# Moving a rank-16 side product out of the up-projection loop of a fused transformer layer, and spreading that loop over four PSUM banks

## The reference, cut to what matters

```python
def qat_lora_linear(x, W, b, A, B):
    Wq = fake_quant_weight(W)              # symmetric 8-bit rounding of the weights
    base = jnp.einsum('bsi,oi->bso', x, Wq) + b
    lora = jnp.einsum('bsr,or->bso', jnp.einsum('bsi,ri->bsr', x, A), B)
    return base + SCALING * lora
h = qat_lora_linear(hidden_states, W_fc, b_fc, A_fc, B_fc)
h = jax.nn.gelu(h, approximate=False)
h = qat_lora_linear(h, W_proj, b_proj, A_proj, B_proj)
...
x = _layernorm(x + attn(x)); x = _layernorm(x + ffn(x))
```

## Time and profile before

| | us |
|---|---|
| three timed runs | 2717.56, 2712.26, 2716.21; median 2716.21 |
| the profiled execution | 2710.28 |
| its span, core 4 (the slowest; the cores have 2699.1 to 2708.6) | 2708.6 |
| PE busy / weight loads / DVE busy / ACT busy in the span | 1614.0 / 757.8 / 1018.9 / 882.2 |
| mean granted TensorE clock, cores 0 to 7 | 0.658 to 0.664 |

### The profile page before, as it was taken

One profiled execution on the slowest core, in us unless ns is written; L12 is line 12 of the kernel. 1 busy time (PEld: TensorE's weight loads), 2 busy tenths in 40 slices (PEclk: granted clock), 3 DMA queues, 4 the chain that ended last, 5 costly groups with the idle time before them and its releaser, 6 DMA issues.

```text
span 2708.6 us, 28767 instructions; the slowest of 8 cores (2699.1 to 2708.6 us)
## 1 busy us (share of the span) xinstructions
PE 1614.0 (60%) x7027; PEld 757.8 (28%) x7038; DVE 1018.9 (38%) x1325; ACT 882.2 (33%) x1229; POOL 74.2 (3%) x119
## 2 busy tenths in 40 slices
PE   0255666677766345412244768677676766777666
PEld 0111222222222112100122435344353433435334
DVE  2266777777777644565544100101000010100101
ACT  0002666666666133512665211112111121211211
POOL 0000000000000000000000000000000000000000
PEclk9667888888797577556555757556575665756557
DMA  5400121211213222201322000000000000000000
GB/s 158 130 1 6 55 66 55 69 55 56 68 51 131 86 75 66 75 0 52 100 96 70 16 1 1 16 0 16 1 1 16 1 16 0 9 8 1 16 1 16
DMA packets 51903, 112.32 MB, mean 41 GB/s; under 512 B 12656, under 2 KB 23408, under 8 KB 50464
## 3 DMA queue, kind: packets, MB, share of 16 engines
q0 software_dynamic: 13552, 50.08, 5.7%
q1 hardware_dynamic: 28688, 37.06, 4.6%
q10 hardware_dynamic: 9504, 23.34, 2.9%
HBM read 97.47 MB, written 8.39 MB: 39 GB/s over the span
## 4 chain that ended last, share of the span: by engine, by line
PE 41%; DVE 21%; ACT 17%; issue 10%; DMA 9%; ACTq 1%; DVEq 1%; SPq 0%; POOLq 0%
PE PSD L313 32%; DVE CL L692 5%; ACT HH L1133 5%; ACT PT L699 4%; PE PSD L1142 3%; DVE MXW L565 3%; ACT QSG L802 3%; PE BIG L608 2%; DMA QSG<-wPRr 2%; DVE CL L685 2%; PE PSD L676 2%; DMA QSG<-wFCr 2%; ACT QTI L806 2%; DMA out<-OST 1%; DMA STG<-xT 1%
## 5 line engine op out<-in xcount | busy, mean ns | idle before, releaser
L313 PE MATMUL PSD<-XT,RTF 128*128 128x256 bf16 x2048 | 482.0, 417 | 1.3 <-DVE UO L1101 1.2
L699 ACT ACTIVATE PT<-CL 128x1024 bf16<-128x1024 f16 (+1 forms) x320 | 310.8, 971 | 184.4 <-DVE CL L685 94.1
L1133 ACT ACTIVATE HH<-PSD,BFCS,SML 128x256 bf16<-128x256 f32 x256 | 144.4, 564 | 672.7 <-PE PSD L313 669.7
L1142 PE MATMUL PSD<-HH,APT 128*16 128x256 bf16 x256 | 94.9, 371 | 397.3 <-ACT HH L1133 353.4
L313 PEld LDWEIGHTS PSD<-XT,RTF 128*128 128x128 bf16 x2048 | 264.6, 140 | 162.4 <-issue 66.7
L1153 DVE TENSOR_SCALAR UPt<-PSD,SML 16x256 bf16<-16x256 f32 x8 | 3.8, 472 | 741.3 <-PE PSD L1142 741.3
L676 PE MATMUL PSD<-QH,KH 96*128 96x512 bf16 (+3 forms) x640 | 199.3, 403 | 114.9 <-DVE CL L685 53.2
L692 DVE TENSOR_SCALAR CL<-PSD 128x1024 f16<-128x1024 f32 x192 | 235.0, 1224 | 74.7 <-PE BIG L608 32.8
L313 PE MATMUL PSD<-HH,RTP 128*128 128x256 bf16 x2048 | 250.7, 284 | 6.4 <-DVE UPt L1153 6.4
L608 PE MATMUL BIG<-PT,VP 128*65 128x512 bf16 (+3 forms) x640 | 196.4, 394 | 68.0 <-ACT PT L699 54.4
L313 PEld LDWEIGHTS PSD<-HH,RTP 128*128 128x128 bf16 x2048 | 202.8, 102 | 45.7 <-issue 8.6
(11 more groups left out here) (148 smaller groups left out, 1294.9 us busy)
## 6 DMA issues: line engine op xcount, KB each, us to landing
STG<-wFCr POOLq DMA_DIRECT2D x32, 512.0 KB, 4.3
STG<-wPRr POOLq DMA_DIRECT2D x32, 512.0 KB, 4.4
out<-OST SPq DMA_DIRECT2D x64, 128.0 KB, 1.9
QSG<-wFCr ACTq DMA_DIRECT2D x27, 256.0 KB, 2.6
QSG<-wFCr POOLq DMA_DIRECT2D x26, 256.0 KB, 2.9
QSG<-wPRr SPq DMA_DIRECT2D x22, 256.0 KB, 3.1
QSG<-wPRr POOLq DMA_DIRECT2D x21, 256.0 KB, 2.8
QSG<-wPRr ACTq DMA_DIRECT2D x21, 256.0 KB, 2.7
```

What stands on the lines that cost most here:

```text
L313: e.matmul(outap, la, ra, start=st, stop=sp),
L699: etok = P.s(lambda e, cs=cs, qw=qw: e.activation(self.PTB[cs][:, 0:qw], self.CLB[cs][:, 0:qw], AF.Exp, scale=ISQ), waits=[ctok, self.pv_t ...
L1133: hh_tok[oc] = P.s(lambda e, oc=oc, sl=sl: e.activation(self.HH[:, TC * oc:TC * oc + TC], self.PSB[sl][:, 0:TC], AF.Gelu, bias=self.BFCS[: ...
L1142: upmm = P.t(lambda e, oc=oc, t=t: e.matmul(self.PSB[2][0:16, 0:TC], self.APT[:, 16 * oc:16 * oc + 16], self.HH[:, TC * oc:TC * oc + TC], ...
```

## The change

In the loop over `oc` the side product's matmul is gone. After the loop it is one group of 32 matmuls, emitted by `mmg`, whose first matmul waits for all 32 Gelu operations. The up-projection's groups go round the banks 0, 1, 4, 5 in place of 0, 1; banks 4 and 5 were last used in phase 4, and the first two groups in them wait for the operations that ended that use (`big_free_ln1`). The down-projection goes round 2, 3, 0, 1 in place of 2, 3.

```diff
@@ -1121,41 +1121,40 @@
             for oc in range(32):
-                sl = oc % 2
+                sl = (0, 1, 4, 5)[oc % 4]
...
-                mmtok = self.mmg(self.PSB[sl][:, 0:TC], parts,
-                                 [qtok_fc[oc], bsf_tok, ufc_tok,
-                                  self.ps_free[sl]] + xt_all + tbar)
+                wfc = [qtok_fc[oc], bsf_tok, ufc_tok,
+                       self.ps_free[sl]] + xt_all + tbar
+                if t == 0 and oc in (2, 3):
+                    wfc.append(self.big_free_ln1)
+                mmtok = self.mmg(self.PSB[sl][:, 0:TC], parts, wfc)
...
-                upw = [hh_tok[oc], self.apt_r]
-                if oc == 0:
-                    upw.append(self.ps_free[2])
-                upmm = P.t(lambda e, oc=oc, t=t: e.matmul(
-                    self.PSB[2][0:16, 0:TC],
-                    self.APT[:, 16 * oc:16 * oc + 16],
-                    self.HH[:, TC * oc:TC * oc + TC],
-                    start=(oc == 0), stop=(oc == 31)),
-                    waits=upw, inc=(oc == 31))
...
-            up_tok = P.v(lambda e: e.tensor_scalar(
-                self.UPt[0:16, 0:TC], self.PSB[2][0:16, 0:TC],
-                self.SML[0:16, 4:5], None, ALU.mult), waits=[upmm])
-            self.ps_free[2] = up_tok
+            sl = 2
+            mmtok = self.mmg(
+                self.PSB[sl][0:16, 0:TC],
+                [(self.APT[:, 16 * f:16 * f + 16], self.HH[:, TC * f:TC * f + TC])
+                 for f in range(32)],
+                [self.apt_r, self.ps_free[sl]] + [hh_tok[oc] for oc in range(32)])
+            up_tok = P.v(lambda e, sl=sl: e.tensor_scalar(
+                self.UPt[0:16, 0:TC], self.PSB[sl][0:16, 0:TC],
+                self.SML[0:16, 4:5], None, ALU.mult), waits=[mmtok])
+            self.ps_free[sl] = up_tok
             for dc in range(8):
-                sl = 2 + dc % 2
+                sl = (2, 3, 0, 1)[dc % 4]
```

## The result

| | before | after |
|---|---|---|
| median of the runs, us | 2714.48 (10 runs, 2709.54 to 2718.55) | 2194.2 (9 runs, 2188.93 to 2247.7) |
| the profiled execution, us | 2710.28 | 2189.92 |
| its span, us | 2708.6 (core 4) | 2188.4 (core 5) |
| PE busy in the span, us | 1614.0 | 1347.4 |

The ratio is 0.8083, with a 95% interval of 0.8067 to 0.8098: 19% less time, forecast at 2193 with a range of 2170 to 2260. Two of the nine runs of the changed kernel took 2247 us, with the cores of one die at a lower granted clock; the ratio leaves them out.

A forecast was written before the change was run, and what follows sets the result against it. PE was taken as bound by a Gelu round trip per chunk and the resulting half clock. Tile 165.4 to 91.4 us: 2710.3 - 518 (seven tiles) - 3.5 (first tile) = 2189, times 1.002 gives 2193; range 2170 to 2260.

The forecast's parts named there:

- exposed last Gelu: Between up-projection and side product: the last Gelu is still waited for once per tile, 1.2 us.
- Spacing of the groups: Up-projection: without waits only matmul spacing binds, 1.17 us a chunk, 37.4 us for 32 chunks.
- The clock: Up-projection: clock rises to full once per tile, cold start costs 2.2 us, giving 39.6; down-projection then starts warm, 30.5.
- C: Rival, up-projection: gaps left by 16-row matmuls keep the clock at half; 37 us more per tile, 2452 us; chance 0.04.
- The side product: After the up-projection: one block of matmuls plus handoff over DVE, 3.4 + 1.17 = 4.6 us per tile.
- lower bound: Side product block: 0.11 us a matmul at full clock, against 0.23 at half clock, which would add 3.7 us.
- The banks: Up-projection: a bank is free after about 1.5 us; two banks give 1.2, so banks 4 and 5 are needed.
- The first tile: Bound by quantising on ACT: last Gelus -8.8, cold block +7.1 or less, down-projection -1.3; -3 to -4 us in all.
- D: Rival, whole kernel: dense matmuls on eight cores get less than half clock, slower than before; at 0.40 about 2865 us; chance 0.02.
- B: Rival, dense stretch of each tile: full clock does not last; 2438 us if it halves after 33 us; chance 0.10.
- the page's figure: Trainium skill's limiter, 13/16 clock with three dense cores: 16.5 us more per tile, about 2315 us.
- rows 9: Profile rows on the clock, read as all eight cores at 1.00 together in the down-projection, no limiter in 33 dense us.

The follow-up runs named there:

- e3: Kernel before with eight added matmuls per group into a bank nobody reads, ahead of the side product, wait for Gelu kept: 2475.8 us, ratio 0.9116.
- e4: Changed kernel with the side product back in the loop, two chunks behind its Gelu: 2217.35 us, ratio 0.8163.
- e6: Changed kernel with every second group, up and down, starting with its 16-row matmul: 2163.64 us, ratio 0.7962.
- e1: Changed kernel with the up-projection's groups on two banks, 0 and 1, instead of four: 2194.75 us, ratio 0.8085.
- e8: Changed kernel with tail inside next tile, first down-projection group ahead of side product, every second group's 16-row matmul first: 2060.07 us, ratio 0.7571.
- e5: Changed kernel with each tile's tail spread over the next tile's up-projection, broadcasts in banks 2 and 3: 2091.86 us profiled, ratio 0.7759.

## Why the prediction was right, step by step

| term, us per tile | forecast | measured | from |
|---|---|---|---|
| up-projection, first matmul to the end of the groups | 39.6 | 39.7 here, 40.4 on average | 1530.02 to 1569.56, + 0.21 |
| exposed last Gelu | 1.2 | 1.0 | 1569.77 to 1570.81 |
| side product and handoff | 4.6 | 4.5 | 1570.81 to 1575.26 |
| down-projection | 30.5 | 30.5 | 1575.26 to 1605.72 |
| tail | 15.5 | 15.4 | 1605.72 to 1621.13 |
| tile | 91.4 | 91.1 here, 91.8 on average | |

*Spacing of the groups.* Right in kind: nothing but matmul spacing binds. 1.19 against 1.17, since in the first group of all the 16-row matmul starts 0.96 us after the first, and in later groups 0.98. That is 0.6 us per tile.

*The clock.* Right. It rises once per tile and stays through the handoffs of 0.97 and 0.80 us. It rises in the second group in the tile of the table and in the third in the six after it, whose up-projections are 0.4 to 1.0 us longer for it; the table's tile is this core's shortest. e3 tests this step by itself: it changes the clock and no dependence, and brought 240 us where its expectation had 236. The case that the 16-row matmuls keep the clock down (C, 2452) is dead by the 1.00 of the up-projection.

*The side product.* The block runs at the lower bound, 0.11 us a matmul. What the prediction did not see is that this holds only inside a block. It spoke of the spacing of the 16-row matmul as a property of that matmul; e4 and e6 show that it is paid at each of the changes of shape that they make.

*The banks.* This step was wrong, at no cost to the sum. The prediction said that two banks give 1.2 us against a need of 1.5 and that this is what banks 4 and 5 are worth. They are worth nothing (e1: 2194.75 against 2194.2). Two errors met: the time given is not one group but one group and the 0.21 us behind the last matmul, 1.41; and the need of 1.47 us was read at half clock, where a matmul's own latency is 0.39 and not 0.28 us, so that some 1.36 remain by this estimate. In e3, at full clock, the same round trip is 1562.93 - 1561.56 = 1.37.

*The first tile.* Forecast -3.5, and -1.3 of it in the down-projection. From the first group to the scaling into UPt it took 1486.0 - 1263.1 = 222.9 before and 1483.7 - 1266.9 = 216.8 after, so -6.1, and -1.3 behind it as forecast. The first tile came out 3.9 us shorter than forecast. The term of the sum that was mis-sized is the block on a cold PE; the rest lies in the quantising. The timeline of ACT and that of PE in the changed kernel:

```profile
1474.82 2.54 ACT L1135 ACTIVATE HH<-PSD,BFCS,SML 128x256 bf16<-128x256 f32 x4
```

```profile
1477.51 6.06 PE L313 MATMUL PSD<-HH,APT 128*16 128x256 bf16 x32 [6.04 <-ACT HH L1135]
1484.36 3.65 PE L313 MATMUL PSD<-HH,RTP 128*128 128x256 bf16 x32 [0.80 <-DVE UPt L1152]
```

The last four Gelus are 0.66 apart and save 8.8 us, as worked out. The block takes 5.7 us to its last start (6.85 less the handoff of 1.17), not 7.1, and the quantising between the first and the 29th Gelu ran 2.4 us shorter (151.4 against 153.8), which no part of the change explains; over the eight cores it is 152.6 to 154.1 before and 151.1 to 153.6 after, so part of this is which core was slowest. The 3.9 us by which the changed kernel's first group comes later in its span than the one of the earlier trace rows lie in the phases ahead of it, which the change does not touch, and in which the cores differ by more: their first Gelus start at 1311 to 1321 us before and at 1310 to 1324 after.

*The sum.* The profiled executions differ by 2710.3 - 2189.9 = 520.4 us, forecast 521.5. That it comes within about 1 us is in part luck: the first tile gave 3.9 us more than forecast, the phases ahead of it took 3.9 back, and tiles 1 to 7 gave some 1.4 us less.

*The rivals.* C and D did not happen. B keeps a part. The stretch at full clock that was 33 us long is now nearly 76 (1530.02 to 1605.72, with some 4 us cold at its start and two short waits in it), and the profiled execution pays nothing for it; the two of 2247 us paid 53, far from B's 2438 and under the 2315 by the page's figure. By the Trainium skill ("TensorE: Matmul & The Clock Gate", Part 1) a die goes to 13/16 of its clock once three of its cores run dense matmuls. The value is what e8's profile shows, 0.81. Whether three cores have to be dense at one moment is open. The prediction took the 1.00 of all eight cores at the same time of their spans as "together", which no profile shows and e8 speaks against. The same holds for the 1.00 of all eight cores in e5: the cores may have run their dense parts at different moments. So rows 9 were weaker evidence against B than the prediction took them for. The longer stretch at 1.00 that the trace before does have, its first 60 us, holds 16 matmuls and says nothing of dense work.

## What to carry to other kernels

A matmul that reads what another engine has only just been given costs its engine a round trip each time, and where these gaps hold the granted clock at one half, about as much again on all the matmuls around it (here 282 and 240 us). Price the two apart: the wait from the idle time in the timeline, the clock by taking the spacing of the same matmuls from a dense stretch of the same profile; a kernel with dummy matmuls in the gap tests the second alone. Then gather matmuls of one shape, and check a bank's round trip at the clock it will have, before adding banks.

## What the runs showed of the hardware that was not expected

- A matmul of 256 columns starts 0.11 us after one with the same number of rows and columns of weights, and 0.21 us after one with another (128 rows to 16 and back; 16 columns to 128). Not every change costs this: in e5 a matmul with 1 row starts 0.12 us after one with 16 (1617.00 to 1617.12). Why some do was not tried. Pairing the 16-row matmuls took 31 us off this kernel (e6 against the changed kernel).
- More work can be faster: 2048 added matmuls took 240 us off (e3).
- The granted clock was 0.81 for 161 us on two cores in dense matmuls, then 1.00 for 155 us on the same work, then 0.81 again (e8), while two cores of the same die show episodes of the same length and distance elsewhere in their spans. What sets it off in some executions and not in others was not tried.
